# An attention, router and expert kernel: output weights centred in set-up, and the projected token scaled and added to x in one VectorE operation

## What is computed

```python
x = L0_attn_x                                                       # 4 x 2048 x 512, float32
x = x + _layernorm(_L0_attn_ref(_layernorm(x), w_qkv, w_out, signs, scales))   # linear attention with random features
x = x + _layernorm(_L0_ffn_ref(_layernorm(x), gate_w, bias, W1, W3, W2, sw1, sw3, sw2))   # 32 experts, 4 per token

def _layernorm(x, axis=-1, eps=1e-05):
    m = jnp.mean(x, axis=axis, keepdims=True)
    v = jnp.var(x, axis=axis, keepdims=True)
    return (x - m) / jnp.sqrt(v + eps)
```

## Time and profile before

| what | value |
|---|---|
| median of three executions | 2131.86 us |
| profiled execution, its own time | 2130.38 us |
| its span, first to last instruction | 2128.0 us |
| busy TensorE, VectorE, ScalarE, GpSimd (share of the span) | 86%, 60%, 44%, 36% |
| instructions on VectorE, ScalarE | 2358, 1243 |
| mean granted TensorE clock | 0.947 of full |
| L984, the scaling of y on ScalarE | 64 times, median 779 ns |

### The profile page before, as it was taken

One profiled execution on the slowest core, in us unless ns is written; L12 is line 12 of the kernel. 1 busy time (PEld: TensorE's weight loads), 2 busy tenths in 40 slices (PEclk: granted clock), 3 DMA queues, 4 the chain that ended last, 5 costly groups with the idle time before them and its releaser, 6 DMA issues.

```text
span 2128.0 us, 31538 instructions
## 1 busy us (share of the span) xinstructions
PE 1829.2 (86%) x11952; PEld 894.7 (42%) x11952; DVE 1280.8 (60%) x2358; ACT 938.7 (44%) x1243; POOL 770.3 (36%) x718
## 2 busy tenths in 40 slices
PE   8999999999969998787888886446888888887785
PEld 5444444444448883232333332313444444443332
DVE  6877676767610000378788888753555555555886
ACT  3444444444346665465656654312333333322343
POOL 0000000000000000126777777874777777751110
PEclk9999999999979999999999998777999999999997
DMA  6544444445368884678778756343898999868983
GB/s 218 187 144 169 149 165 157 157 170 184 120 176 212 211 211 113 165 205 235 202 218 237 204 187 200 119 164 82 179 213 220 233 240 231 199 136 234 328 300 137
DMA packets 188695, 404.98 MB, mean 190 GB/s; under 512 B 33668, under 2 KB 71940, under 8 KB 171920
## 3 DMA queue, kind: packets, MB, share of 16 engines
q1 hardware_dynamic: 83040, 222.38, 36.8%
q10 hardware_dynamic: 68640, 124.26, 16.2%
q0 software_dynamic: 36864, 56.32, 13.4%
HBM read 237.03 MB, written 177.08 MB: 195 GB/s over the span
## 4 chain that ended last, share of the span: by engine, by line
DVE 23%; PE 18%; DMA 6%; issue 6%; POOL 4%; ACT 4%; SPq 1%; POOLq 0%; DVEq 0%; ACTq 0%
PE s_gates L1474 6%; PE s_ups L1474 6%; DVE s_xT L1607 4%; DVE s_y L1622 3%; DMA s_spread<-share_dram 3%; POOL slot_dram L1252 3%; PE s_y L895 2%; DVE s_heads L1092 2%; DVE s_h L1597 1%; DVE s_stats L1646 1%; DVE s_x L1665 1%; DVE s_at_hl L1096 1%; ACT s_parts L1533 1%; ACT s_gate L1527 1%; PE s_logits L864 1%
## 5 line engine op out<-in xcount | busy, mean ns | idle before, releaser
L258 PE MATMUL s_proj<-s_xT,keep_wqkv 128*128 128x512 f16 x1536 | 344.2, 379 | 0.0
L1252 POOL DMA_INDIRECT slot_dram<-keep_filled,keep_slots x256 | 277.7, 1085 | 104.6 <-issue 74.0
L1417 POOL DMA_INDIRECT acc_dram<-s_y,s_slot x128 | 200.4, 1566 | 113.3 <-DVE s_y L1622 68.5
L895 PE MATMUL s_y<-keep_wo,s_at_hl 128*128 128x512 f16 x768 | 195.5, 409 | 40.1 <-ACT s_z L984 40.1
L258 PEld LDWEIGHTS s_proj<-s_xT,keep_wqkv 128*128 128x128 f16 x1536 | 149.1, 98 | 180.2 <-issue 12.6
L1527 ACT ACTIVATE s_gate<-s_gates 128x512 f32<-128x512 f32 x96 | 57.1, 597 | 292.7 <-PE s_ups L1474 247.3
L338 POOL TENSOR_SCALAR s_rstd<-s_mv 128x4 f32<-128x4 f32 x16 | 16.0, 1000 | 462.6 <-DVE s_mv L353 462.6
L1597 DVE SCALAR_TENSOR_TENSOR s_h<-s_gate,s_ups 128x512 f32<-128x512 f32 x96 | 65.8, 686 | 187.8 <-ACT s_gate L1527 187.8
L235 PE MATMUL s_proj<-keep_wqkv,s_xT 128*128 128x512 f16 x768 | 172.9, 382 | 4.9 <-DVE keep_wqkv L404 4.9
L963 ACT ACTIVATE s_phi<-s_logits 128x1024 f32<-128x1024 f32 x128 | 131.5, 1027 | 92.0 <-PE s_logits L864 91.3
L674 ACT ACTIVATE s_phi<-s_logits 128x1024 f32<-128x1024 f32 x128 | 131.1, 1024 | 86.2 <-PE s_logits L695 86.2
(11 more groups left out here) (164 smaller groups left out, 3241.5 us busy)
## 6 DMA issues: line engine op xcount, KB each, us to landing
s_x<-x_in SPq DMA_DIRECT2D x32, 1024.0 KB, 10.4
qk_dram<-s_hl ACTq DMA_DIRECT2D x32, 1024.0 KB, 7.1
keep_ahead<-qk_dram SPq DMA_DIRECT2D x48, 512.0 KB
acc_dram<-s_zero SPq DMA_DIRECT2D x17, 1024.0 KB, 8.9
v_dram<-s_v ACTq DMA_DIRECT2D x16, 1056.0 KB, 4.0
s_v<-v_dram SPq DMA_DIRECT2D x16, 1056.0 KB, 11.1
s_spread<-share_dram SPq DMA_DIRECT2D x64, 256.0 KB
x_dram<-s_x ACTq DMA_DIRECT2D x16, 1024.0 KB, 7.8
```

Of the source, the lines that this page charges most:

```text
L258: mm = nc.tensor.matmul(out[:, 512 * b:512 * b + 512], left, right, start=(c == 0 and i == 0), stop=(c == EC - 1 and i == 2))
L895: mm = nc.tensor.matmul(y[m % 2][:], at_hl[n % 2][:, s, c, a * P:(a + 1) * P], keep["wo"][:, w, c, :], start=(c == 0 and i == 0), stop=(c ...
L1252: nc.gpsimd.indirect_dma_start(out=io["slot"], out_offset=bass.IndirectOffsetOnAxis(ap=slots[n % 2][:, a * K + j:a * K + j + 1], axis=0), ...
L1417: nc.gpsimd.indirect_dma_start(out=io["acc"], out_offset=bass.IndirectOffsetOnAxis(ap=slot[e % RING][:, a, 0:1], axis=0), in_=y[e % 2][:, ...
```

## The change

Set-up gets `centre_wo` on VectorE, behind the fourth part of the second token group: the mean over the 512 output features is taken from the loaded `w_out` by a reduction and one operation over 128x2048. ScalarE's `make_wo_high` waits for that instead of the load.

In the attention and routing stage `make_z` and the tile `z` go. `add` on VectorE computes x plus y times rstd from PSUM in one operation; it stands in the step that `make_z` had, and so every later part has one step of delay less: 84 steps instead of 85. `project` waits for the add of tile m-2 instead of its z. `make_shift` computes the one bias that is left, for the second layer norm.

```diff
+            def centre_wo():
+                dve.wait_ge(w_out_loaded, 16)
+                nc.vector.tensor_reduce(wo_mean[:], w_out[:], AX.X, ALU.add).then_inc(wo_summed, 1)
+                dve.wait_ge(wo_summed, 1)
+                nc.vector.scalar_tensor_tensor(out=w_out[:], in0=wo_mean[:].unsqueeze(2).broadcast_to([P, EC, E]),
+                                               scalar=-1.0 / E, in1=w_out[:], op0=ALU.mult,
+                                               op1=ALU.add).then_inc(wo_centred, 1)
...
+                if n == 1 and j == 3:
+                    centre_wo()
...
             def make_wo_high():
-                act.wait_ge(w_out_loaded, 16)
+                act.wait_ge(wo_centred, 1)
...
-        PROJECT, MEASURE, SCALE, ADD, SPLIT, TURN, COPY, GATE = 8, 9, 10, 11, 12, 13, 14, 14
-        SCORE, CHOOSE, PLACE, WEIGH, FILL, SEND = 18, 18, 19, 19, 21, 21
+        PROJECT, MEASURE, ADD, SPLIT, TURN, COPY, GATE = 8, 9, 10, 11, 12, 13, 13
+        SCORE, CHOOSE, PLACE, WEIGH, FILL, SEND = 17, 17, 18, 18, 20, 20
...
                 if m >= 2:
-                    pe.wait_ge(z_ready, m - 1)
+                    pe.wait_ge(x1_ready, m - 1)
...
-            def make_z(m):
-                k = m % 2
-                act.wait_ge(shift_ready, m + 1)
-                if m >= 2:
-                    act.wait_ge(x1_ready, m - 1)
-                nc.scalar.activation(z[k][:], y[k][:], ACT.Identity, bias=shift[k][:, 0:1],
-                                     scale=rstd[k][:, 0:1]).then_inc(z_ready, 1)
...
-                nc.vector.scalar_tensor_tensor(out=shift[k][:], in0=mv[k][:, :, 0], scalar=-1.0, in1=rstd[k][:],
+                nc.vector.scalar_tensor_tensor(out=shift[k][:], in0=mv[k][:, 1, 0:1], scalar=-1.0, in1=rstd[k][:, 1:2],
                                                op0=ALU.mult, op1=ALU.mult).then_inc(shift_ready, 1)
...
             def add(m):
                 n, a = m // A, m % A
-                dve.wait_ge(z_ready, m + 1)
+                dve.wait_ge(rstd_ready, m + 1)
                 if a == 0:
                     dve.wait_ge(x_loaded[n % XS], 16 * (n // XS) + 16)
-                nc.vector.tensor_tensor(x[n % XS][:, a, :], x[n % XS][:, a, :], z[m % 2][:], ALU.add).then_inc(x1_ready, 1)
+                nc.vector.scalar_tensor_tensor(out=x[n % XS][:, a, :], in0=y[m % 2][:], scalar=rstd[m % 2][:, 0:1],
+                                               in1=x[n % XS][:, a, :], op0=ALU.mult, op1=ALU.add).then_inc(x1_ready, 1)
...
-                if 0 <= s - SCALE < UNITS:
-                    make_shift(s - SCALE)
+                if 0 <= s - ADD < UNITS:
+                    make_shift(s - ADD)
```

More of the change, by code:

```diff
@@ L772, in attend_and_route_programs @@
         x = [t.sb(f"x{r}", [P, A, E]) for r in range(XS)]
-        z = t.pair("z", [P, E])
         xn = t.pair("xn", [P, A, E])
@@ L776, in attend_and_route_programs @@
         stats = t.pair("stats", [P, 2, 6])
-        mv, rstd, shift = t.pair("mv", [P, 2, 2]), t.pair("rstd", [P, 2]), t.pair("shift", [P, 2])
+        mv, rstd, shift = t.pair("mv", [P, 2, 2]), t.pair("rstd", [P, 2]), t.pair("shift", [P, 1])
         power, eps = t.sb("power", [P, 2]), t.sb("eps", [P, 2])
@@ L992, in normalize @@
                     act.wait_ge(turned_ready, A * (n - 1))
-                nc.scalar.activation(xn[n % 2][:, a, :], x[n % XS][:, a, :], ACT.Identity, bias=shift[k][:, 1:2],
+                nc.scalar.activation(xn[n % 2][:, a, :], x[n % XS][:, a, :], ACT.Identity, bias=shift[k][:],
                                      scale=rstd[k][:, 1:2]).then_inc(xn_ready, 1)
```

23 lines of the change are left out of this document (10 added, 13 removed).

## The result

The changed kernel takes **2155.4 us** (median of four runs, 2152.59 to 2156.59) against 2131.5 us before: ratio 1.0114, 95% interval [1.0096, 1.0132]. The forecast was 2115, its range ended at 2130. The profiled execution took 2152.59 us, its span 2150.8. Medians leave out two executions that lie far off the others of their kernel, one of e13 (6379 us) and one of before (2170 us).

The account below looks back on a forecast made before the run. No engine is full; a group is a loop through VectorE, TensorE and ScalarE, VectorE its longest link. Set-up +0.8, groups -9.6, one step less -6.7, sends -1.5: -17.0 us, so 2113.4, by the median 2115 us; range 2094 to 2130.

Parts of the forecast that it names:

- Add: VectorE's add, now scaled with one PSUM operand, takes 0.743 us, 0.06 us more each, 0.24 a group.
- Scaling of y gone, divide's wait gone: ScalarE loses a 0.78 us operation a step, worth nothing by itself; VectorE's divide wait goes, minus 0.7 us.
- Low copy: VectorE's low copy of the transposed tile waits 2.5 us a group against 2.2, plus 0.3.
- The share: VectorE's share waits for the denominators' round trip 0.9 us a group instead of 1.6, minus 0.7.
- Groups: Groups of four steps in the steady loop fall from 31.8 to 31.0 us, over twelve groups 9.6 us.
- the regrouping gives nothing: Rival, chance 0.24: waits in the loop only change places, groups stay at 31.8 us, total 2124.5 us.
- Set-up: Two new VectorE operations in set-up make VectorE 4.6 us later but cost only 0.8 us.
- One step less and the sends: At the stage's end, last rstd one step earlier, minus 6.7 us; GpSimd's sends beside the add shorter, minus 1.5 us.
- The slower rival: Chance 0.15: the loop through GpSimd sets the pace, groups take 33.8 us, total 2148 us by the median.

Follow-up runs that it names:

- e13: Kernel before with fused add, centring and norm chain one step earlier, and the rows store one step earlier too, at kind 0: 2144.4 us, ratio 1.0077.
- e1: Changed kernel with only the 1 MB store of the normalized rows issued one step later, where the kernel before had it: 2129.8 us, ratio 1.0018.
- e4: Changed kernel with fill issued ahead of the share in VectorE's step, stores left as changed: 2124.0 us, ratio 0.9985.
- e9: Changed kernel with the rows store and the x1 store each one step later, turned store left as changed: 2127.2 us, ratio 0.9997.
- e6: Kernel before with only the set-up centring of the output weights and ScalarE's wait on it added, loop untouched: 2134.2 us, ratio 1.0014.
- e10: Changed kernel with the rows store and the turned store each one step later, x1 store left as changed: 2144.4 us, ratio 1.0081.
- e11: Changed kernel with fill ahead of the share, the two centring instructions in separate steps and the rows store one step later: 2150.5 us, ratio 1.0111.
- e14: Kernel before with only the turned store one step later, issued right behind the x1 store: 2129.1 us, ratio 1.0012.

## Why the prediction was wrong

Point by point, by its own terms:

- **Add**: right. 0.744 us, 64 times, against a forecast of 0.743. The 0.065 us more for a PSUM source do not show on top of it.
- **Scaling of y gone, divide's wait gone**: right, 0 in groups 4 to 16 for 0.65.
- **Low copy**: forecast 2.5 us a group, 2.73 measured: right in size, but in four places a group and not in three (37 waits in the 9.4 groups of the stretch; before, 20 in 10).
- **The share**: this is the step that failed, "0.9 instead of 1.6". The prediction counted what VectorE does beside the round trip and took the trip's length as given, 4.97 us, from one group (the mean of groups 4 to 16 was 5.59). It is 8.09 in the mean now, and the share waits 3.66 us. The change moves three stores of 1 MB by a step, and through the shorter steps the loads of the queries; the prediction counted none of them. e1 moves one back and the loss goes.
- **What the share's wait costs**: the prediction saw that the fill would stand behind it and gave that no price but in a rival. That the order counts is shown by e4 (fill ahead of it: 2124.0); e13 beside e1 gives the price, 0.94 us a microsecond against 0.35.
- **Groups**: 31.0 forecast, 33.87 measured, 1.93 more than before: the share waits 1.90 more, the low copy 0.23 more, the divide 0.65 less, the add takes 0.24 more, and 0.2 stay open. Without the rows store in the trip (e1, e9) 32.2 and 31.6, so even then at most 0.3 of the 0.8 us came: nearest to the rival "the regrouping gives nothing", though the runs of both stay above its 2124.5 and their load is still late in some groups.
- **Set-up**: mis-sized, 0.8 forecast (its own rows, 4.6 less 3.5, give 1.1) and 5.2 at the end of the stage. The 4.6 us of VectorE were right; the next wait was sought at TensorE's products at 125 us, where it was indeed 0.2, but the one that counts came 9 us later, by way of the next group's statistics, and the clock then fell to 0.58 for 2.5 us. In the run's time 3 us (0 to 6), by e6.
- **One step less and the sends**: -8.2 forecast, -4.8 measured. The first send after an rstd takes 1.03 instead of 1.51 us, as forecast; but in the last steps GpSimd waits 0.73 us for an aggregate and 1.01 for the slots.
- **The slower rival** had the sign, not the mechanism. The shift waits only 0.3 us a group for rstd, while GpSimd waits 5.4 for the slots: its loop is not the bound.

Of the cause, shown are the late load (trace, e1), the big transfers ahead of the small ones (row DMA and queues of after and e10; for the second leg by e11's divide and issue times) and fill's place (e4, with e13 in support). That the queries' nearness to den is what e14 lacks rests on e10's queues, on issue times and on the last groups; no run moved the queries alone.

## What to carry to other kernels

A step taken out of a pipeline moves every transfer that is issued relative to it, and shorter steps move those that only wait for progress. Before such a change is priced, lay the issues of all queues over the short round trips through DRAM that an engine waits for, and ask whether the DMA is still full when each small transfer is due. And look at what stands behind a wait on its engine: the same wait cost 0.35 of itself here where the work that other engines wait for stood a step later, and 0.94 where it stood behind it.

## What the runs showed of the hardware

A load of 32 KB on SP's queue, issued 1.0 us behind a 1 MB store on ScalarE's, let VectorE go on 5.35 us after its issue instead of 1.84: the other queue was no shelter. The Trainium skill, DMA: Bandwidth & Descriptors, section Queues, rings and completion order, says that a transfer's semaphore increment lands only after all earlier writes of that DMA engine, across its queues; by that rule the load is seen only once the store is done, and the trace agrees in the order (store at work until 1096.5, share at 1099.0). But the queues show more than a late semaphore: from its issue at 1093.65 to 1096 the load moved no packet, while the store moved nearly all of its own. So it did not get a share of the bandwidth either. Why its packets stood back stays open.

The store of 1 MB in that group moved at about 400 GB/s, alone but for small transfers. In e10, with queries, x1 and turned rows, 3.5 MB from 11.7 us ahead of den, the engines were full until 2.5 us behind it.

These two stops cost TensorE twice: behind the one of 5.67 us in the shown group its clock had a mean of 0.53 from 1103 to 1108, and in set-up behind one of 2.66 us 0.58 for the next 2.5 us.
